# Passage from attention to experts: first early rows split beside the last heads, the last batch's rows on VectorE, late rows found over three tile steps, two gathers ahead of stores

## Chip, cores and metric

One core of a Trainium2 chip runs the whole kernel. The metric is the device time of one execution, in microseconds. Three runs of the kernel before gave 1546.72, 1548.99 and 1550.43 us; the median is 1548.99.

## What is computed

```python
# x, ctx: (16, 256, 256) float32; 8 heads of 128; 8 experts with 1024 hidden columns, 2 per token
x = x + tanh(g_xattn) * perceiver_attention(ctx, layernorm(x))   # keys: 256 context rows and 256 latent rows
n = layernorm(x)                                                 # eps 1e-5
gates = (n @ Wg + bg) / (1 + 1e-6)
weights, indices = top_k(gates, 2);  weights = softmax(weights)
h = silu(n @ W1[e] + b1[e]);  y = h @ W2[e] + b2[e]              # of the two chosen experts e
x = x + tanh(g_ffn) * sum(weights * y)
```

All of it is float32. A product on TensorE is made of three passes over parts that were split before: `hi` (rounded to the fast format, on ScalarE) and `lo` (the rest, on VectorE or POOL). Each operand of a product therefore passes ScalarE and then VectorE before TensorE can take it.

## The kernel before, in words

Each engine has its program in order (`sync`, `gpsimd`, `scalar`, `tensor`, `vector`), written out by hand; they meet at semaphores alone, so where an instruction stands in its engine's order is what sets when it runs.

**Attention.** 16 batches of 8 heads make `STEPS` = 128 steps i (L54), and two more drain them. In a step TensorE makes the scores of head i (`scores`), transposes the probabilities of head i-1 (`turn_probs`), projects head i-2 (`out_proj`) and works through units (`unit`): k, q and v parts of the next head, o of the last. VectorE reads maxima, the low halves `pt_lo`, kt, qt, v, ot; ScalarE the exponentials and high halves; POOL normalises the probabilities (L881). Behind the last head of a batch b the work on its rows is spread over the steps of the next batch: `residual` (h=1), `norm_rows` on POOL (h=1), the transposes t and gates g, `largest`, `choose`, `weigh` (h=6), `find_places` (h=7) on VectorE and `list_tokens` (h=7) on POOL, which writes the tokens' numbers into lists of each expert in DRAM with four indirect DMAs. The normalised rows go to `xhat_rows` in DRAM.

**Experts.** The pairs of token and expert are worked off in 40 tiles t: 31 wide ones of 256 rows (`WIDE`) and 9 of 128. The first five (`EARLY`) belong to the two fullest experts and take only rows of batches 0 to 13, so that they are known before attention ends; the others, the late ones, need the last batches. A wide tile has four steps n (`step_of(t)` = 4t). In step n TensorE does `hidden(n)` (12 products, W1) and `out(n - 2)` (12 products, W2); ScalarE does `silu(n)` and `hi_h(n)`, VectorE `lo_h(n)`. A tile's rows are gathered by POOL (`gather`, one DMA of 128 rows for each half), transposed by TensorE (`turn_x`, at the steps of `X_TURN`), split by ScalarE and VectorE (`hi_x`, `lo_x`, at those of `X_SPLIT`), and their weights taken (`take_weights`). When a tile is through, VectorE makes `finish` (bias, and a scaling of each 128x256 half by the weights, L1716) and POOL adds the rows to the output with an indirect DMA (`scatter`, L906); each scatter waits for the one before it (`s_add`).

**Beside it.** W2 of all experts is loaded (SP) and split in 32 pieces (`w2_hi`, `w2_lo`), the first four in steps 127 and 128 of attention (`W2_STEPS`), the others over the first expert steps; W1 of a tile is split two steps ahead of use (`w1_hi`, `w1_lo`). In steps 4 to 14 the last batch is dealt with: transposes t (step 4, waiting for the rows of `norm_rows(15)` on POOL), gates g, `choose`, r (step 7), `find_places(15)`, then `list_tokens(15)` on POOL, `find_rows` on VectorE (step 8, with `weigh(15)`), which says for each late row of tiles its expert and its place in the lists; POOL fetches the `names` (tokens) of the late rows, TensorE turns them at step 14 (`NAMES_STEP`), and VectorE writes the `token` table, on which `gather(5)`, the first late tile, waits.

**Around the change.** TensorE's order at attention step 127: `scores(127)`, `turn_probs(126)`, `out_proj(125)`, `turn_x(0)`, unit o(126); at step 128: `hidden(0)` (waits for `lo_x(0)`), `turn_probs(127)`, `out_proj(126)`, `hidden(1)`, o(127), `hidden(2)`; then `out_proj(127)`, `turn_x(1)`, `out(0)`, steps n from 3. POOL's order: at step 127 `normalise(127)`, `list_tokens(14)`; behind the loop `gather(2)` (two DMAs), `norm_rows(15)`, then by t: `gather(3)`, `scatter(0,0)`, `list_tokens(15)`; `scatter(0,1)`, `gather(4)`, `names`, `scatter(1,0)`; `scatter(1,1)`, `gather(5)`, and so on. A gather of tile t waits until tile t-2 is transposed and its weights are taken. In POOL's `norm_rows`, L821 is the variance with its epsilon, L793 the power to -1/2, L796 the sign, L799 the two instructions that write the rows. `turn_x(5)` stands at step 19, with `hi_x(5)` and `lo_x(5)`; step 20 is the first that uses them.

```python
X_TURN = ({step_of(t) + (t < WIDE) for t in range(1, N_TILES - 1) if t + 1 != EARLY} | {step_of(EARLY) - 1})
X_SPLIT = {step_of(t) + 2 for t in range(WIDE) if t + 1 != EARLY} | {step_of(EARLY) - 1}
```

## Time and profile before

| | |
|---|---|
| median of three runs | 1548.99 us (1546.72 to 1550.43) |
| the profiled execution's own time | 1550.09 us |
| its span, first to last instruction | 1548.4 us |
| mean granted TensorE clock | 0.993 of full speed |
| busy in the span | PE 97%, DVE 72%, ACT 62%, POOL 39% |
| attention | to about 1101 us; experts behind it |

The span holds all instructions of one execution; its own time lies 1.7 us above it. The granted clock has two levels in this trace, 1.0 (2.4 GHz) and 0.5 (1.2 GHz). Line numbers L... are those of the kernel before; products of all kinds stand at L181 to L183, so they are told apart by the tiles that they write: `score`, `ring` (units), `proj`, `ph` (hidden), `py` (out), `px` (turned rows; the first tile's go to `routing`). "Idle before" names what the profile saw end last. xt_lo is `lo_x`, ht_lo `lo_h`, w_lo `w2_lo`, w1s_lo `w1_lo`, and py with ht_lo is `out`.

### The profile page before, as it was taken

How to read it: one execution, taken by the hardware profiler on the slowest of the kernel's cores; microseconds unless marked ns; L12 is line 12 of the kernel's file. 1: busy time of each engine (PE TensorE's matmuls, PEld its weight loads, DVE VectorE, ACT ScalarE, POOL GpSimd, SP SyncE). 2: the span in 40 equal slices, each digit the busy share in tenths (PEclk: the TensorE clock that was granted, in tenths of full speed). 3: DMA queues.
4: the chain of work that ended last, by engine and by line, in shares of the span. 5: the costliest groups of instructions: out<-in, count | busy, mean ns of one | idle time of the engine just before them, and what ended most of it. 6: DMA issues, size and time to landing. Idle time of an engine off the chain costs nothing. (4 is left out here: it accounts for less than half of the span.)

```text
span 1548.4 us, 29904 instructions
## 1 busy us (share of the span) xinstructions
PE 1501.3 (97%) x10410; PEld 1383.4 (89%) x10410; DVE 1112.3 (72%) x2687; ACT 954.0 (62%) x2060; POOL 603.0 (39%) x714
## 2 busy tenths in 40 slices
PE   6999998999999999999999999999899999999997
PEld 5888897988989888898888889888889999999996
DVE  6777775777777777777777777677686666666685
ACT  5655654555555655655555555655677777777775
POOL 5323423233343333334243343233455444445442
PEclk9999999999999999999999999999999999999999
DMA  4000100000000000000000000012855545555553
GB/s 148 19 21 8 21 8 21 8 21 29 8 22 8 22 27 2 29 8 22 8 21 29 8 22 8 8 29 82 226 121 133 130 125 152 132 127 147 140 171 83
DMA packets 57823, 91.13 MB, mean 59 GB/s; under 512 B 8521, under 2 KB 44774, under 8 KB 57550
## 3 DMA queue, kind: packets, MB, share of 16 engines
q1 hardware_dynamic: 41710, 70.19, 14.1%
q0 software_dynamic: 15824, 18.98, 6.9%
q8 instruction: 88, 1.44, 0.4%
q14 instruction: 57, 0.47, 0.1%
q10 hardware_dynamic: 144, 0.05, 0.0%
HBM read 70.91 MB, written 18.29 MB: 58 GB/s over the span
## 5 line engine op out<-in xcount | busy, mean ns | idle before, releaser
L881 POOL TENSOR_SCALAR probs<-probs,rsum 128x512 f32<-128x512 f32 x256 | 174.2, 692 | 531.8 <-DVE rsum L1553 517.5
L1093 ACT ACTIVATE pt_hi<-turn 128x512 fp32r<-128x512 f32 x256 | 139.7, 597 | 238.5 <-PE turn L1239 238.5
L906 POOL DMA_INDIRECT out_rows<-yo,token x71 | 120.6, 1699 | 206.4 <-DMA out_rows<-yo,token 149.2
L1670 DVE TENSOR_TENSOR ht_lo<-hs,ht_hi 128x512 fp32r<-128x512 f32 x142 | 98.2, 692 | 119.8 <-ACT ht_hi L1058 114.9
L1547 DVE TENSOR_REDUCE smax<-score 128x1 f32<-128x512 f32 x256 | 169.8, 685 | 12.9 <-PE score L183 11.6
L992 ACT ACTIVATE probs<-score,nbias 128x512 f32<-128x512 f32 x256 | 173.7, 688 | 4.2 <-DVE nbias L1549 4.1
L1049 ACT ACTIVATE hs<-ph,vecs 128x256 f32<-128x256 f32 (+1 forms) x284 | 114.8, 460 | 95.1 <-PE ph L183 86.2
L1782 DVE TENSOR_TENSOR pt_lo<-turn,pt_hi 128x512 fp32r<-128x512 f32 x256 | 164.2, 682 | 9.3 <-ACT pt_hi L1093 9.2
L181 PE MATMUL py<-w_hi,ht_lo 128*128 (+1 forms) x568 | 163.1, 287 | 3.9 <-DVE ht_lo L1670 3.9
L182 PE MATMUL py<-w_lo,ht_hi 128*128 (+1 forms) x568 | 161.0, 283 | 0.0
L183 PE MATMUL py<-w_hi,ht_hi 128*128 (+1 forms) x568 | 161.0, 283 | 0.0
L181 PE MATMUL ring<-pt_hi,v_lo 128*128 128x256 f32 x512 | 146.4, 286 | 9.4 <-DVE kt_lo L1450 7.7
L980 ACT ACTIVATE kt_hi<-ring,vecs 128x512 fp32r<-128x512 f32 x128 | 88.6, 692 | 94.4 <-PE ring L183 93.7
L181 PE MATMUL ph<-xt_hi,w1s_lo 128*128 128x256 f32 x496 | 141.4, 285 | 4.6 <-DVE xt_lo L1648 4.5
L183 PE MATMUL ring<-pt_hi,v_hi 128*128 128x256 f32 x512 | 145.1, 283 | 0.0
L182 PE MATMUL ring<-pt_lo,v_hi 128*128 128x256 f32 x512 | 144.9, 283 | 0.0
L1450 DVE SCALAR_TENSOR_TENSOR qt_lo<-ring,vecs,qt_hi 128x256 fp32r<-128x256 f32 x128 | 61.8, 483 | 107.6 <-ACT qt_hi L982 104.9
L183 PE MATMUL ph<-xt_hi,w1s_hi 128*128 128x256 f32 x496 | 139.0, 280 | 0.0
L182 PE MATMUL ph<-xt_lo,w1s_hi 128*128 128x256 f32 x496 | 138.7, 280 | 0.0
L1239 PEld LDWEIGHTS turn<-ident,probs 128*128 128x128 f32 x1024 | 121.4, 142 | 17.4 <-POOL probs L881 0.3
L1239 PE MATMUL turn<-ident,probs 128*128 128x128 f32 x1024 | 134.4, 275 | 0.0
L1450 DVE SCALAR_TENSOR_TENSOR kt_lo<-ring,vecs,kt_hi 128x512 fp32r<-128x512 f32 x128 | 95.8, 748 | 51.0 <-ACT kt_hi L980 43.1
(247 smaller groups left out, 4708.8 us busy)
## 6 DMA issues: line engine op xcount, KB each, us to landing
w_raw<-in_L_ffn_W SPq DMA_DIRECT2D x45, 1024.0 KB, 8.4
xhat_rows<-rows SPq DMA_DIRECT2D x16, 264.0 KB, 2.2
x_raw<-in_x SPq DMA_DIRECT2D x16, 256.0 KB, 3.0
c_raw<-in_ctx SPq DMA_DIRECT2D x16, 256.0 KB, 3.1
out_rows<-x SPq DMA_DIRECT2D x16, 256.0 KB, 2.2
xg<-xhat_rows,token POOLq DMA_INDIRECT x71, 5.0
out_rows<-yo,token POOLq DMA_INDIRECT x71
v_raw<-in_L_xattn_Wkv SPq DMA_DIRECT2D x2, 512.0 KB, 8.3
```

The costliest lines, as they stand in the source:

```text
L181: pe.matmul(out, ll, rh, start=start, stop=False, **kw)
L182: pe.matmul(out, lh, rl, start=False, stop=False, **kw)
L183: return pe.matmul(out, lh, rh, start=False, stop=stop, **kw)
L881: last = pool.tensor_scalar(probs[n % 2][:, t, :], probs[n % 2][:, t, :], rsum[:, n % 2, t:t + 1], 1.0, ALU.mult, ALU.mult)
L906: pool.indirect_dma_start(out=A["out"], out_offset=bass.IndirectOffsetOnAxis(ap=token[:, u:u + 1].bitcast(U32), axis=0), in_=yo_of(t)[:, s ...
L992: act.activation(probs[n % 2][:, t, :], score[t][:, :], ACT.Exp, scale=SCALE, bias=nbias[:, n % 2, t:t + 1], accum_out=ssum[:, n % 2, t:t ...
L1049: last = act.activation(by_step(hs[n % N_HS], t)[:, g, :], by_step(ph[n % N_PH] if t < WIDE else turned_of(n), t)[:, g, :], ACT.Silu, bias ...
L1093: act.activation(pt[0][:, 2 * t:2 * t + 2, :], turn[t][:, :].rearrange("p (j i) -> p j i", j=2), ACT.Copy).then_inc(s_pthi, 1)
L1239: last = pe.transpose(turn[t][:, j * T + q * P:j * T + (q + 1) * P], probs[n % 2][:, q, (2 * t + j) * P:(2 * t + j + 1) * P], ident[:, :])
L1450: dve.scalar_tensor_tensor(out=lo[:, :], in0=part, scalar=bias, in1=hi[:, :].bitcast(F32), op0=ALU.add, op1=ALU.subtract).then_inc(s_read, 1)
L1547: own.mark(dve.tensor_reduce(smax[:, n % 2, t:t + 1], score[t][:, :], AX_X, ALU.max))
L1782: dve.tensor_tensor(pt[1][:, 2 * t:2 * t + 2, :], turn[t][:, :].rearrange("p (j i) -> p j i", j=2), pt[0][:, 2 * t:2 * t + 2, :].bitcast(F ...
```

## The change

1. On TensorE `turn_x(0)` moves ahead of `turn_probs(126)`; on ScalarE `hi_x(0)` and the first two `w2_hi` move ahead of the high half of o(126); on VectorE `lo_x(0)` moves ahead of the low half of o(126). `find_places(14)` moves from attention step 127 to 128, behind `lo_h(0)`, and the weights of tiles 0 and 1 are taken at step 128.
2. The last batch's rows are normalised by VectorE, inside its order behind `residual(15)` and `lo_h(1)`; POOL keeps only the power, behind `gather(2)`. A semaphore `ve_last` is new.
3. `find_rows` becomes `count_rows` (step 8) and `find_late_rows` (step 9); `weigh(15)` moves to step 10.
4. On POOL `gather(3)` and `gather(4)` both stand ahead of `scatter(0,0)`, and `list_tokens(15)` and the fetch of `names` ahead of `scatter(0,1)`.
5. `turn_x(5)`, `hi_x(5)` and `lo_x(5)` move from step 19 to step 18.

```diff
@@ -129,8 +129,8 @@
 NAMES_STEP = 14
 
 
-X_TURN = ({step_of(t) + (t < WIDE) for t in range(1, N_TILES - 1) if t + 1 != EARLY} | {step_of(EARLY) - 1})
-X_SPLIT = {step_of(t) + 2 for t in range(WIDE) if t + 1 != EARLY} | {step_of(EARLY) - 1}
+X_TURN = ({step_of(t) + (t < WIDE) for t in range(1, N_TILES - 1) if t + 1 != EARLY} | {step_of(EARLY) - 2})
+X_SPLIT = {step_of(t) + 2 for t in range(WIDE)}
 
 
 def plan_units():
@@ -481,6 +481,7 @@
         s_whi = sem("weights_hi")
         s_wlo = {"dve": sem("weights_lo_dve"), "pool": sem("weights_lo_pool")}
         s_media0, s_zt1 = sem("kvt0_media"), sem("zt0_media")
+        s_ve_last = sem("ve_last")
         s_ve0, s_rs0 = sem("ve0"), sem("rs0")
         s_z0, s_zt0, s_lat0, s_kvl0 = sem("z0_latents"), sem("z0_turned"), sem("zt0_latents"), sem("kvt0_latents")
         s_tg = sem("tanh_gate")
@@ -938,7 +939,8 @@
 
             for s in range(SUB):
                 gather(2, s)
-            norm_rows(B - 1)
+            pool.wait_ge(s_ve_last, 1)
+            pool.tensor_tensor(rs_c[:, 0:TT], ve["c"][:, 0:TT], minus_half[:, 0:TT], ALU.pow).then_inc(s_rsc, 1)
             for t in range(1, N_TILES + 1):
                 if WIDE + N_XG <= t + N_GN < N_TILES:
                     gather(t + N_GN, 0)
@@ -947,19 +949,21 @@
                 if t + N_XG == EARLY:
                     pool.wait_ge(s_rowst[1], 16 * (B // 2))
                     pool.wait_ge(s_token, 1)
-                if t + N_XG < min(N_TILES, WIDE + N_XG):
-                    for s in range(subs(t + N_XG)):
-                        gather(t + N_XG, s)
-                if t == 2:
+                for later in {1: (3, 4), 2: ()}.get(t, (t + N_XG,)):
+                    if later < min(N_TILES, WIDE + N_XG):
+                        for s in range(subs(later)):
+                            gather(later, s)
+                if t == 1:
+                    scatter(0, 0)
+                    list_tokens(B - 1)
                     pool.wait_ge(s_row, 1)
                     pool.wait_ge(s_listed, 16 * TOP * TT * B)
                     pool.indirect_dma_start(
                         out=names[0:LATE_SUB, 0:P], out_offset=None, in_=dram["lists"],
                         in_offset=bass.IndirectOffsetOnAxis(ap=row[0:LATE_SUB, :].bitcast(U32), axis=0),
                     ).then_inc(s_names, 16)
-                scatter(t - 1, 0)
-                if t == 1:
-                    list_tokens(B - 1)
+                if t > 1:
+                    scatter(t - 1, 0)
             pool.wait_ge(s_add, 16 * ROWS)
 
         @program("scalar")
@@ -1101,6 +1105,10 @@
                 if i < STEPS:
                     exp(i, 0)
                     exp(i, 1)
+                if i == STEPS - 1:
+                    hi_x(0)
+                    for q in W2_STEPS[i]:
+                        w2_hi(q)
                 for u in units:
                     if u[0] != "k":
                         hi_part(*u)
@@ -1117,13 +1125,13 @@
                 if i % H == E_STEP and 1 <= i // H < B:
                     exp_gap(i // H - 1)
                 if i == STEPS - 1:
-                    hi_x(0)
                     e = expert_of(act, 0)
                     act.wait_ge(s_x2st[0], 16 * (B // 2))
                     act.wait_ge(s_rowst[0], 16 * (B // 2))
                     act.activation(warm[:, :], iota8[:, :], ACT.Silu).then_inc(s_warm, 1)
-                for q in W2_STEPS.get(i, ()):
-                    w2_hi(q)
+                if i == STEPS:
+                    for q in W2_STEPS[i]:
+                        w2_hi(q)
             piece = W2_BEFORE
             for n in range(1, FIRST_N):
                 t, j = TILE_OF[n]
@@ -1358,14 +1366,14 @@
                     scores(i)
                 if i == STEPS:
                     hidden(0)
-                if 1 <= i <= STEPS:
-                    turn_probs(i - 1)
-
-                if STEPS - 1 <= i <= STEPS:
-                    out_proj(i - 2)
                 if i == STEPS - 1:
                     wait_read(pe, order[number["o", STEPS - 1] - 2])
                     turn_x(0)
+                if 1 <= i <= STEPS:
+                    turn_probs(i - 1)
+
+                if STEPS - 1 <= i <= STEPS:
+                    out_proj(i - 2)
                 if i == STEPS:
                     hidden(1)
                 for u in steps[i]:
@@ -1583,7 +1591,7 @@
                 for i, n in enumerate(HOME_SUB):
                     own.mark(dve.tensor_scalar(begin[:, i:i + 1], begin[:, i:i + 1], float(n), None, ALU.add))
 
-            def find_rows():
+            def count_rows():
 
                 def do(instruction):
                     own.mark(instruction)
@@ -1609,6 +1617,14 @@
                                             op0=ALU.mult, op1=ALU.subtract))
                 own.mark(dve.tensor_tensor(begin[:, ODD:ODD + E], begin[:, 0:E], length[:, 0:E], ALU.add))
                 do(dve.tensor_reduce(wide_rows[:, :], length[:, 0:E], AX_X, ALU.add))
+
+            def find_late_rows():
+
+                def do(instruction):
+                    own.mark(instruction)
+                    own.wait()
+
+                own.wait()
                 do(dve.tensor_scalar(wide_rows[:, :], wide_rows[:, :], -1.0, float(LATE_WIDE), ALU.mult, ALU.add))
                 do(dve.tensor_scalar(length[:, GAP:GAP + 1], wide_rows[:, :], 0.0, None, ALU.max))
                 do(dve.tensor_tensor_scan(end[:, :], length[:, :], zero[:, :], 0.0, ALU.add, ALU.add))
@@ -1785,11 +1801,14 @@
                             .then_inc(s_ptlo, 1)
                 if i == STEPS:
                     lo_h(0)
+                    find_places(B - 2)
                 for u in steps[i]:
                     if u[0] in "kq":
                         read_unit(*u)
                 if i < STEPS:
                     reciprocal_sum(i)
+                if i == STEPS - 1:
+                    lo_x(0)
                 for u in steps[i]:
                     if u[0] in "vogr":
                         read_unit(*u)
@@ -1804,7 +1823,7 @@
                 if 1 <= b < B:
                     for at, part in ((R_STEP, residual), (G_STEP, largest), (E_STEP, choose), (W_STEP, weigh),
                                      (L_STEP, find_places)):
-                        if h == at:
+                        if h == at and i != STEPS - 1:
                             part(b - 1)
                 if i == HOME_STEP:
                     find_home()
@@ -1813,15 +1832,21 @@
                     dve.tensor_copy(token[:, 0:EARLY_SUB], early_names[:, :]).then_inc(s_early_token, 1)
                 if W1_STEP <= i < W1_STEP + PARTS:
                     w1_lo(0, i - W1_STEP)
-                if i == STEPS - 1:
-                    lo_x(0)
                 for q in W2_STEPS.get(i, ()):
                     w2_lo(q)
-                if i == STEPS - 1:
+                if i == STEPS:
                     take_weights(0)
                     take_weights(1)
             residual(B - 1)
+            dve.wait_ge(s_mvc, B)
+            dve.tensor_scalar(ve["c"][:, 0:TT], mv_c[:, 0:TT, 1], 1.0, EPS, ALU.mult, ALU.add).then_inc(s_ve_last, 1)
             lo_h(1)
+            dve.wait_ge(s_rsc, B)
+            dve.wait_ge(s_rowst[(B - 1) % 2], 16 * ((B - 1) // 2))
+            for t in range(TT):
+                last = dve.tensor_scalar(rows[(B - 1) % 2][:, t, 0:D], x2[(B - 1) % 2][:, t, :], mv_c[:, t, 0:1],
+                                         rs_c[:, t:t + 1], ALU.subtract, ALU.mult)
+            last.then_inc(s_xn, 1)
             piece = W2_BEFORE
             for n in range(2, FIRST_N):
                 t, j = TILE_OF[n]
@@ -1842,7 +1867,10 @@
                     largest(B - 1)
                     choose(B - 1)
                 if n == 8:
-                    find_rows()
+                    count_rows()
+                if n == 9:
+                    find_late_rows()
+                if n == 10:
                     weigh(B - 1)
                 if n == NAMES_STEP:
                     fill_tables()
```

## Rows read from the trace of the kernel before

**Rows 1.** The page: busy time and share of the engines; the gathers' median to landing.

```profile
PE 1501.3 (97%) x10410; PEld 1383.4 (89%) x10410; DVE 1112.3 (72%) x2687; ACT 954.0 (62%) x2060; POOL 603.0 (39%) x714
...
xg<-xhat_rows,token POOLq DMA_INDIRECT x71, 5.0
```

**Rows 2.** Stretches: width, busy us (instructions) of PE, PEld, DVE, ACT, POOL; clock, DMA.

```profile
1092.00:1095.40 3.40, 3.40 (x19) 3.40 (x18) 2.17 (x11) 1.44 (x3) 2.79 (x3) 0.50 1.09 350
1163.80:1167.00 3.20, 3.20 (x16) 3.20 (x16) 1.92 (x5) 1.52 (x4) 2.90 (x2) 0.50 0.30 85
1200.00:1300.00 100.00, 100.00 (x852) 100.00 (x851) 62.90 (x133) 73.04 (x146) 47.79 (x34) 1.00 0.49 130
1130.00:1142.70 12.70, 9.57 (x77) 8.96 (x77) 12.44 (x31) 8.21 (x18) 8.63 (x5) 1.00 0.58 67
```

**Rows 3.** Waits of TensorE, 1050 to 1200 us: total, times, longest.

```profile
PE ph L181 <- DVE xt_lo L1648: 4.5, 2, 2.8
...
PE py L181 <- DVE ht_lo L1670: 1.6, 1, 1.6
PE px L1263 <- DMA xg<-xhat_rows,token: 1.4, 1, 1.4
PE ring L1206 <- POOL rows L799: 1.3, 1, 1.3
```

**Rows 4.** Timeline of TensorE: start, duration in us; in brackets the idle time before.

```profile
1090.81 0.39 PE L181 MATMUL ph<-xt_hi,w1s_lo 128*128 128x256 f32 x1 [2.77 <-DVE xt_lo L1648]
...
1106.23 0.28 PE L181 MATMUL ph<-xt_hi,w1s_lo 128*128 128x256 f32 x1
...
1111.72 0.63 PE L1263 MATMUL px<-ident,xg 128*128 128x128 f32 x4
...
1167.40 0.60 PE L1263 MATMUL px<-ident,xg 128*128 128x128 f32 x4
```

**Rows 5.** Timeline of ScalarE around the last heads.

```profile
1088.08 0.48 ACT L984 ACTIVATE ot_hi<-ring,vecs 128x256 fp32r<-128x256 f32 x1 [1.50 <-PE ring L183]
...
1090.47 1.14 ACT L1023 ACTIVATE w_hi<-w_raw 128x512 fp32r<-128x512 f32 x2
```

**Rows 6.** Timeline of VectorE: places, residual and moments, scaling of rows.

```profile
1090.00 0.17 DVE L1507 CAST place<-placef 128x4 int32<-128x4 f32 x1
...
1101.52 0.69 DVE L1532 TENSOR_TENSOR y<-proj,bo 128x512 f32<-128x512 f32 x1
...
1103.82 0.25 DVE L1417 BATCH_NORM_AGGREGATE mv_c<-stats_c 128x2 f32<-128x6 f32 x2
...
1119.43 0.62 DVE L1716 TENSOR_SCALAR yo<-yo,wcol 128x256 f32<-128x256 f32 x2
...
1136.63 1.28 DVE L1716 TENSOR_SCALAR yo<-yo,wcol 128x256 f32<-128x256 f32 x2
```

**Rows 7.** Timeline of POOL: gather(2), the power, gather(4), a store.

```profile
1097.43 0.96 POOL L892 DMA_INDIRECT xg<-xhat_rows,token  x1 [0.30 <-issue]
...
1104.77 0.72 POOL L793 TENSOR_TENSOR rs_c<-ve_c,minus_half 128x2 f32<-128x2 f32 x1
...
1131.24 1.00 POOL L892 DMA_INDIRECT xg<-xhat_rows,token  x1 [0.30 <-issue]
...
1160.08 1.58 POOL L906 DMA_INDIRECT out_rows<-yo,token  x1 [8.17 <-DMA out_rows<-yo,token]
```

**Rows 8.** POOL's DMA queue in 1102-1106, 1106-1108, 1108-1112, 1112-1116, 1162-1166: packets, MB, share.

```profile
q0 software_dynamic: 39, 0.11, 23.7%
...
q0 software_dynamic: 59, 0.16, 19.6%
...
q0 software_dynamic: 5, 0.01, 0.8%
...
q0 software_dynamic: 95, 0.27, 17.9%
...
q0 software_dynamic: 232, 0.40, 52.8%
```

More of the change, by code:

```diff
@@ L1360, in _ @@
                     hidden(0)
+                if i == STEPS - 1:
+                    wait_read(pe, order[number["o", STEPS - 1] - 2])
+                    turn_x(0)
                 if 1 <= i <= STEPS:
@@ L1365, in _ @@
                     out_proj(i - 2)
-                if i == STEPS - 1:
-                    wait_read(pe, order[number["o", STEPS - 1] - 2])
-                    turn_x(0)
                 if i == STEPS:
@@ L1792, in _ @@
                     reciprocal_sum(i)
+                if i == STEPS - 1:
+                    lo_x(0)
                 for u in steps[i]:
@@ L1815, in _ @@
                     w1_lo(0, i - W1_STEP)
-                if i == STEPS - 1:
-                    lo_x(0)
                 for q in W2_STEPS.get(i, ()):
                     w2_lo(q)
-                if i == STEPS - 1:
+                if i == STEPS:
                     take_weights(0)
```

## The prediction

> **What bounds the kernel now.** I read the page's busy shares first: TensorE is busy for 97% of the span [rows 1]. The table of stretches comes next. In it the reader is to see where TensorE has no reserve: from 1200 us on it is busy all the time at the full granted clock [rows 2], so that every microsecond won before that comes off the end, and nothing else in the kernel has to be looked at. The waits of TensorE between 1050 and 1200 us then name what is there to win in the passage to the experts: 4.5 us in two waits for the low half of turned rows (2.8 and 1.7), 1.6 for a low half of hidden values, 1.4 for a gather, 1.3 for the last batch's normalised rows on POOL [rows 3]. Behind the 2.8 and the 1.7 the granted clock was 0.50, that is 1.2 GHz instead of 2.4, for 3.4 and 3.2 us [rows 2]: 1.7 and 1.6 us more of lost time. In all some 12 us, of which the change aims at each piece. The timelines of the engines say what each piece hangs on; the steps n of the experts are about 2.9 us each.
>
> **First early rows split beside the last heads.** In before, TensorE ended its last but one attention unit at 1088.0 and stood until 1090.81 for lo_x(0) [rows 4]. ScalarE had been free since 1086.6 (1088.08 less 1.50 idle), but read the turned rows only behind ot_hi, 0.59 long [rows 5]. Now the transposes (0.4) stand ahead of the probabilities' and push ScalarE's two exponentials back by about 0.25. hi_x(0) runs 1086.8 to 1087.35 and lo_x(0), 0.7 long, ends at 1088.05. Step 0 starts at 1088.1: 2.7 us won, and the 1.7 of half clock behind it with it. The two w2 pieces that ScalarE now does ahead of ot_hi (1.14 [rows 5]) move that by 0.3, hidden by the transposes ahead of the projection that reads it. So TensorE is through with attention 4.4 us earlier, at about 1096.7 instead of 1101.1.
>
> **What is late next.** find_places(14), which before ended at 1090.2 [rows 6], now stands behind lo_h(0), which needs step 0, the last head's two pt_hi on ScalarE (behind its table load, ready at 1090.3), the activation (0.85) and hi_h(0) (0.64). Durations without a group are those of the same timelines' neighbouring lines. I get 1093.0 for lo_h(0)'s start, 1093.55 for its end and, with 1.15 for the eight small instructions, 1094.7: 4.5 us later than before. POOL has list_tokens(14) and gather(2) queued behind it and issues six DMAs, which before took from 1090.2 to 1098.4 [rows 6, 7]; now they end at 1102.9, and only then can POOL take the power of the new s_ve_last. The power (0.72 [rows 7]) gives rs_c at 1103.7. VectorE meanwhile: low half of the last head 1095.4, two w2 pieces 1.2, four take_weights 1.1, residual and moments 2.5 (1101.52 to 1104.07 [rows 6]), the spread 0.2, lo_h(1) 0.6, done by 1101.4. It then **stands 2.3 us in the new wait for rs_c**, with lo_x(1), lo_h(2) and, through them, TensorE behind it. out(1) needs lo_h(1): a wait of about 1.4. The two row instructions on VectorE replace 2.9 us of POOL, but their price is not shown as such: the nearest row is the scaling of two 128x256 tiles with a per-partition scalar, 0.62 for both while POOL was idle and 1.28 while POOL issued DMAs [rows 6]. POOL goes on to gather(3) here, so I take 1.28 and keep 0.62 as the other end. Rows are ready at 1105.0, lo_x(1) at 1105.7; step 4 starts then, against 1106.23 [rows 4], with a wait of about 2.7. Of 4.4 us only 0.5 is left.
>
> From step 4 to turn_x(2) took 5.5 us (1106.23 to 1111.72), 1.3 of them the wait for POOL's rows [rows 3, 4], which is gone: 4.2, so turn_x(2) is wanted at 1109.9. Two things push it back. The waits of 1.4 and 2.7 lie like those ahead of the first half-clock stretch, which was 1.7: between nothing and 1.7. And gather(2): it is issued 4.5 us later, the last part at 1101.9. Before, it was issued by 1097.43, and POOL's queue moved 0.11 MB in 1102 to 1106 and 0.16 in 1106 to 1108, together the 0.27 MB of its two tiles: 10 us to land. In 1108 to 1112 that queue got 0.8% of the engines while the w2 loads kept them full [rows 8]. Bounds for its landing: 1106.5, if the loads are through by then (5 us from issue, the median of all 71 gathers [rows 1]), and 1112 (the same 10 us). I take 1110 and, with part of the half clock, turn_x(2) at 1110.7: **1.0 us won**.
>
> The Trainium skill, DMA: Bandwidth & Descriptors, Queues, rings and completion order, says that each DMA engine goes round the queues that have work, a packet at a time. By that gather(2) would get turns beside the loads and land without a wait of TensorE; POOL's 0.8% against the loads' fill does not look like equal turns, so the measurement has the word. By the rule turn_x(2) would start 0.8 earlier than in my sum, which is the first step of case (a) below.
>
> **Late rows over three pairs, gathers ahead of stores.** VectorE has no time free here: it is busy 12.44 of 12.70 us from 1130 to 1142.7 [rows 2]. Steps 8 to 10 hold the same instructions in another order, so the waits of 1.6 (low half) and 1.4 (gather(4), issued at 1131.24 behind the lists and a store [rows 3, 7], now some 12 us sooner) go, but I expect new ones of 0.9 and 2.2 at steps 12 and 13, where VectorE's w1 piece is late behind weigh and finish. Only 0.6 us that VectorE stood because of the gather is really won: the token table comes 1.0 + 0.6 = 1.6 us sooner. The names are fetched ahead of one store instead of behind it and have room. POOL's queue past them: four stores wait for each other, about 5 us each, so the tile behind the names is still on time.
>
> **The first late tile turned at step 18.** Its wait of 1.7 and the 1.6 of half clock behind it go, provided gather(5) has landed: its issue hangs on the tokens, 10 us ahead of step 18, enough for the 5 us that it takes. TensorE would thus reach turn_x(6) 1.6 + 3.3 = 4.9 us sooner than 1167.40 [rows 4]. But gather(6) stands behind a store that waited 8.17 us for the one before it, in the stretch of w1 and b2 loads [rows 7]; tokens, loads and stores all shift together by 1.6. In 1162 to 1166 POOL's queue moved 0.40 MB, one store (0.13) and gather(6) (0.27) [rows 8]: it had landed at about 1166.3, 1.1 ahead of its use. So turn_x(6) can start at 1164.7, **2.7 us won**, with TensorE idle 2.2 before it. Waits of 1.4 and 1.6 left the clock alone, 1.7 and 2.8 didn't [rows 2, 3]: this one is at the edge, and I charge half of 1.6.
>
> **Sum.** 2.7 - 0.8 = 1.9, say 2.0 us off the profiled execution, 1550.09 (span 1548.4 and 1.7 around it): 1548.1. That execution is 1.1 above the median of the three runs, 1548.99, so I forecast 1547.0. About 0.2% (3 us) is what a measurement of this kernel can tell from no change.
>
> **Rivals.** (a) *The passage clears*, over 3.1 us: loads are through before gather(2) wants the engines, no half-clock stretch is left, and POOL is free of gather(2) sooner than I have it. turn_x(2) is then at 1109.3 (rows at the short price, 0.62), 2.4 won, the tokens 3.0 sooner, turn_x(6) 4.1 won; with a faster store chain up to 6. That gives 1545 to 1543. For it: the w2 loads keep their old start, and six of POOL's DMAs leave their way until 1095. Against: VectorE's queue is full [rows 2], and hides no part of a wait. (b) *Slower*: gather(2), issued behind find_places(14), is caught by the starved stretch of 1108 to 1112 [rows 8] and lands at 1115.6, as the next gather did (0.27 MB in 1112 to 1116 [rows 8]). turn_x(2) is then 3.9 late; the 0.6 and 1.1 are still won, and a half clock behind the wait costs 1.6: 3.8 slower, 1552.8. It decides from a landing past about 1111.7, and costs over 0.2% from 1114.8 on. (c) *It doesn't do what it says*: the rows on VectorE wait for POOL anyhow, so moving them brings nothing; that is in my sum (0.5 of 4.4 left), and with both half-clock stretches kept the whole change brings 0 to 1: 1548 to 1549.
>
> **Chances.** My forecast with (c) 0.57, (a) 0.33, (b) 0.10, counted as slower throughout. The range takes the whole of the first (1545.9 to 1549.8), most of (a) and the near end of (b): 1543.6 to 1550.2.
>
> **What would show it.** Right: first matmul of step 0 at about 1088.1 behind a wait below 0.2; place of batch 14 at about 1094.7; a wait of VectorE for POOL's rs_c of 2 us or more, and of TensorE for lo_x(1) ahead of step 4; the wait for rows on POOL gone; a wait of 2 us for a gather ahead of turn_x(6). Wrong: no wait of VectorE for rs_c, turn_x(2) before 1108 or behind 1113, or turn_x(6) before 1163.

## The result, and the profile after

The changed kernel takes 1556.61 us (median of four runs, 1556.17 to 1558.17), the kernel before beside it 1547.86. The ratio is 1.0057, with a 95% interval of 1.0041 to 1.0073: 8.7 us slower, where 2 us faster were forecast and 1550.2 was the end of the range. The profiled execution took 1558.17 us with a span of 1556.5, 8.1 us over the span of before; its mean granted clock is 0.991 against 0.993.

The busy line of the page, then the waits of TensorE between 1050 and 1200 us (total, times, longest), of the changed kernel; they answer to [rows 1, 3]:

```profile
PE 1501.4 (96%) x10410; PEld 1385.0 (89%) x10410; DVE 1111.0 (71%) x2690; ACT 950.7 (61%) x2060; POOL 599.3 (39%) x710
```

```profile
PE px L1271 <- DMA xg<-xhat_rows,token: 10.0, 2, 6.3
PE ph L181 <- DVE xt_lo L1664: 2.9, 2, 2.7
PE ph L181 <- DVE w1s_lo L1670: 2.0, 1, 2.0
PE ring L181 <- issue: 1.7, 2, 1.0
PE py L181 <- DVE ht_lo L1686: 1.1, 1, 1.1
```

TensorE's work is the same; the waits changed hands. Those that the change aimed at went: the rows on POOL (1.3), the low hidden half (1.6) and both waits for turned rows (4.5 together). In their place stand one of 2.65 for lo_x(1), one of 2.0 for w1s_lo, and 10.0 us for gathers, where it was 1.4.

The timeline of TensorE shows where. Until the last heads each instruction of this trace stands 1.72 us earlier than in the one of before (the same matmul at 1084.67 and 1086.39), so 1.72 is to be added before a time is put beside [rows 4]; such a time is called aligned below.

```profile
1084.67 0.35 PE L181 MATMUL ring<-pt_hi,v_lo 128*128 128x256 f32 x1 [1.04 <-issue]
...
1094.36 0.60 PE L1271 MATMUL px<-ident,xg 128*128 128x128 f32 x4
...
1099.06 0.38 PE L181 MATMUL py<-w_hi,ht_lo 128*128 128x256 f32 x1 [1.09 <-DVE ht_lo L1686]
...
1103.40 0.58 PE L181 MATMUL ph<-xt_hi,w1s_lo 128*128 128x256 f32 x1 [2.65 <-DVE xt_lo L1664]
...
1112.73 0.44 PE L1271 MATMUL px<-ident,xg 128*128 128x128 f32 x2 [3.63 <-DMA xg<-xhat_rows,token]
...
1162.90 0.69 PE L1271 MATMUL px<-ident,xg 128*128 128x128 f32 x2 [6.32 <-DMA xg<-xhat_rows,token]
...
1174.12 0.38 PE L1271 MATMUL px<-ident,xg 128*128 128x128 f32 x2
```

The gap ahead of step 0 is gone. turn_x(2) (1112.73) starts at 1114.45 aligned, 2.7 later than before, behind 3.63 us for gather(2). turn_x(5) (1162.90, now at step 18) waits 6.32 for gather(5), where before it did not wait at all. turn_x(6) (1174.12) is at 1175.84 aligned: 8.4 later, nearly the whole loss (the last tiles, behind 1461 us, add some 1.3). Behind the waits the clock fell to its lower level, as the stretches show (columns as in [rows 2]):

```profile
1103.40:1106.40 3.00, 3.00 (x14) 3.00 (x15) 2.95 (x5) 0.00 (x0) 1.36 (x1) 0.50 0.82 76
1162.90:1167.50 4.60, 4.60 (x22) 4.60 (x23) 1.07 (x5) 1.46 (x4) 1.71 (x2) 0.50 0.25 29
```

They cost 1.5 and 2.3 us. Behind turn_x(2) it was 0.58 over 3.3 us as well. POOL's timeline in the changed kernel has both lost gathers in it:

```profile
1093.17 1.08 POOL L859 DMA_INDIRECT expert_lists<-ids,place  x1 [6.57 <-DVE place L1515]
...
1098.43 1.45 POOL L893 DMA_INDIRECT xg<-xhat_rows,token  x1 [0.30 <-issue]
1100.19 0.96 POOL L893 DMA_INDIRECT xg<-xhat_rows,token  x1 [0.30 <-issue]
1101.17 0.74 POOL L943 TENSOR_TENSOR rs_c<-ve_c,minus_half 128x2 f32<-128x2 f32 x1
...
1130.65 1.12 POOL L859 DMA_INDIRECT expert_lists<-ids,place  x1 [0.30 <-issue]
1138.10 1.70 POOL L961 DMA_INDIRECT names<-expert_lists,row  x1 [6.33 <-DMA expert_lists<-ids,place]
1140.10 1.62 POOL L907 DMA_INDIRECT out_rows<-yo,token  x1 [0.30 <-DVE yo L1732]
1144.77 3.53 POOL L907 DMA_INDIRECT out_rows<-yo,token  x1 [3.05 <-DMA out_rows<-yo,token]
1151.09 1.77 POOL L907 DMA_INDIRECT out_rows<-yo,token  x1 [2.79 <-DMA out_rows<-yo,token]
1153.16 1.03 POOL L893 DMA_INDIRECT xg<-xhat_rows,token  x1 [0.30 <-issue]
```

gather(2) goes out behind the four list writes of batch 14. Further down, POOL stands 6.33 us in the wait ahead of the names; then come three stores, one behind the other, and only then gather(5), at 1153.16. SP's two loads of w1 and the one of b2 went out at 1149.82 to 1151.55, ahead of it.

### The profile page after: what moved, and what is told of

The parts are those of the page before. It is cut to its first block, busy times and chain, and to the rows that moved or that the text cites. A ratio compares the mean times of both kernels' runs of the same rounds, so it can differ in the third digit from the quotient of the medians.

```text
span 1556.5 us, 29904 instructions
## 1 busy us (share of the span) xinstructions
PE 1501.4 (96%) x10410; PEld 1385.0 (89%) x10410; DVE 1111.0 (71%) x2690; ACT 950.7 (61%) x2060; POOL 599.3 (39%) x710
## 4 chain that ended last, share of the span: by engine, by line
PE 81%; DVE 8%; DMA 4%; ACT 3%; issue 2%; POOL 0%; another core or an unknown queue 0%; ACTq 0%; DVEq 0%; POOLq 0%
PE ring L181 12%; PE ring L182 12%; PE ring L183 12%; PE turn L1247 6%; PE score L181 4%; PE score L183 3%; PE score L182 3%; PE py L181 3%; PE ph L181 3%; PE ph L183 3%; PE ph L182 3%; PE py L182 3%; PE py L183 3%; DMA out_rows<-yo,token 2%; PE proj L182 2%
```

## The experiments

The parts of the change are called by number: 1, first early rows beside the last heads (with the places of batch 14 moved to step 128); 2, the last batch's rows on VectorE; 3, late rows over three pairs; 4, POOL's order (gathers ahead of stores, names ahead of scatter(0,1)); 5, tile 5 turned at step 18. They ran on four chips, four experiments to a chip, beside runs of the kernel before on the same chip (medians 1547.19, 1554.09, 1558.56, 1551.39 us): only the ratios are compared, 0.001 being 1.55 us. A ratio is of medians, a trace shows one execution. In five kernels the profiled one lies 2.5 us or more off the median: places back (1551.48 against 1554.01), part 4 alone (1555.78 against 1562.86), gather(2) first (1557.24 against 1560.24), loads split with POOL's order as before (1559.74 against 1556.57) and writes behind on the changed kernel (1549.46 against 1552.88). There the waits quoted need not be those of the median.

### Two places undone

**Store first.** The changed kernel with one store ahead of the wait for the names:

```diff
-                if t >= 2 and subs(t - 2) == 2:
+                if t >= 3 and subs(t - 2) == 2:
                     scatter(t - 2, 1)
...
                 if t == 1:
                     scatter(0, 0)
                     list_tokens(B - 1)
+                    scatter(0, 1)
                     pool.wait_ge(s_row, 1)
```

> The changed kernel with one edit: scatter(0,1) goes out behind the four list writes and ahead of the wait for the names, as before the change. Theory (store chain): in the changed kernel POOL stood 6.3 us for the list writes to land with scatter(0,1) queued behind that wait, and as each store waits for the one before it, gather(5) went out at 1153.2, 5 us behind the token table, in the w1 and b2 loads. Then gather(5) now goes out within 1 us of the token table, the wait ahead of turn_x(5) falls from 6.3 to under 1.5 us, and the time from 1556.6 to 1549 to 1551. Rival (gather(5) is late because of the loads alone, or because it is wanted a step sooner): the wait stays at 4 us or more and the time above 1554.

Ratio 1.0054 (1.0034 to 1.0073). The wait went as expected, and the gain did not come. gather(5) is issued at 1148.46, ahead of the loads (1149.46), and turn_x(5) has no wait at all; but the wait is passed on:

```profile
1168.66 1.11 PE L1272 MATMUL px<-ident,xg 128*128 128x128 f32 x4 [3.47 <-DMA xg<-xhat_rows,token]
```

gather(6) is now the late one, with half clock behind it: turn_x(7) comes 14.6 us after turn_x(6), not 11.75.

**Places back.** find_places(14) at step 127 again:

```diff
-                    find_places(B - 2)
...
-                        if h == at and i != STEPS - 1:
+                        if h == at:
```

> The changed kernel with one edit: find_places(14) stands at attention step 127 again, behind the low half of o(126) and behind lo_x(0). Theory (late places): the list writes and gather(2) go out 4 to 4.5 us sooner, VectorE's wait for the power of rs_c (2.95) and TensorE's for lo_x(1) (2.65) nearly go, and the wait for gather(2) (3.6) falls under 1; the wait ahead of turn_x(5) stays at 6 us, so the time falls by 3 to 5 us, to 1552 to 1554. Rival (gather(2) is held by the w2 loads whenever it goes out): the wait for gather(2) stays above 2.5 us and the time within 1.5 us of 1556.6.

Ratio 1.0039 (1.0023 to 1.0055). The waits for rs_c and for lo_x(1) nearly went (0.6 us instead of 2.95, and 0.26 instead of 2.65), as the prediction's sum has them. The wait for gather(2) stayed, 2.99 us. This trace stands 2.01 us ahead of the changed kernel's at the last heads; with that added, the list writes went 4.4 us earlier and gather(2) only 2.3, and it landed 4.1 earlier: 19.9 us behind the first list write (1086.72 to 1106.58), where it was 19.6 in the changed kernel (1093.17 to 1112.73). The landing follows the writes and not its own issue.

**Both.** The two edits together:

> Both edits, store first and places back. If the two causes are separate and are all that went wrong, the waits for gather(2) and gather(5) are both under 1.5 us and the time is 1544 to 1547, below the 1547.9 of the kernel before. If something else in the change costs time, it stays above 1548.5.

Ratio 1.0032 (1.0018 to 1.0047); turn_x(2) waits 3.07, and turn_x(5) again 5.96. One of POOL's stores took 6.94 us to issue here (1136.94) and pushed gather(5) behind the loads once more.

**gather(3) held.** Whether gather(3), which now follows at once, takes the engines from gather(2):

```diff
+                if t == 1:
+                    pool.wait_ge(s_px, 3)
                 for later in {1: (3, 4), 2: ()}.get(t, (t + N_XG,)):
```

> The changed kernel with one edit: POOL issues gather(3) only when turn_x(2) has run, instead of right behind gather(2). Theory (late places alone): no difference, the wait ahead of turn_x(2) stays at 3.6 us and the time at 1556 to 1557. Rival (gather(3), two DMAs of 128 rows just behind it, slows gather(2)): that wait falls by 2 us or more and the time by 2 to 4.

Ratio 1.0064 (1.0043 to 1.0085), turn_x(2) waits 2.94: 0.7 us less, and nothing gained. gather(3) is not the cause.

### Each part alone, on the kernel before

The edits are those of the diff.

> The kernel before with part 1 of the change alone (first early rows split beside the last heads, find_places(14) at step 128). Theory (the split wins 4.4 us and gives them back, and more, because the list writes and gather(2) follow find_places(14)): gather(2) lands some 19 us behind batch 14's places, as in the first four runs, so that TensorE waits for it 3 us or more ahead of turn_x(2); the wait for POOL's rows grows from 1.3 to 3 or 4 us. Time 1548.5 to 1551. Rival (the split is a gain, the loss is in the other parts): 1543 to 1546.

Part 1: ratio 1.0025 (1.0009 to 1.0041). The gap ahead of step 0 is gone, turn_x(2) waits 3.78 for gather(2), and TensorE 3.19 for POOL's rows. So the part that wins 2.8 us at its own place loses 3.9 over all.

> The kernel before with part 4 alone (gather(3), gather(4), scatter(0,0), lists, names, scatter(0,1) on POOL). Theory (a store behind the names' wait): names go out 6 us behind the last list write as before, scatter(0,1) 5 us later than before, and with it the chain of stores, so that gather(5) goes out about 1151 instead of 1147.2, behind the w1 and b2 loads; TensorE waits for it 2 to 5 us at step 19, the wait of 1.4 for gather(4) is gone: 1549 to 1552. Rival (POOL's order is neutral or a small gain): 1545.5 to 1547.5.

Part 4: ratio 1.0048 (1.0032 to 1.0064). Names behind a wait of 6.79 us, gather(5) issued at 1153.74 behind the loads of 1148.57, turn_x(5) waits 3.88 though it stands at step 19 still. This trace is of the fastest execution of seven, so the 7.4 us of the ratio are not all in it.

> The kernel before with part 2 alone (the last batch's rows on VectorE). The wait for POOL's rows (1.3) goes, VectorE waits 1 to 1.5 us for the power, and step 4 starts up to 1 us later: within 1 us of the kernel before by every theory, 1546 to 1548.5. More than 2 us slower would put a cause here that I have not seen.

Part 2: ratio 0.9995 (0.9983 to 1.0006): nothing, as rival (c) had it for this piece. The wait for POOL's rows went and the one for gather(4) fell to 0.8; 0.3 and 0.6 us came elsewhere.

> The kernel before with part 5 alone (first late tile turned and split at step 18). gather(5), issued ahead of the loads, has landed by step 18, the wait of 1.7 for lo_x(5) goes; TensorE then waits 2 to 4 us for gather(6) ahead of turn_x(6), whose landing is unchanged. Theory (gathers set the pace, not the split): within 1.5 us of the kernel before, 1545.5 to 1548.5. Rival (the step is wanted too early and gather(5) has not landed): a wait for gather(5) of 2 us or more and 1549 or more.

Part 5: ratio 1.0045 (1.003 to 1.0061). The wait ahead of lo_x(5) is gone with its half clock, and turn_x(6) waits 9.88 us. POOL's timeline says why: the first of gather(6)'s two DMAs took 6.02 us to issue, with no transfer under way from 1164 to 1168.

```profile
1161.68 6.02 POOL L892 DMA_INDIRECT xg<-xhat_rows,token  x1 [0.30 <-issue]
1168.00 0.97 POOL L892 DMA_INDIRECT xg<-xhat_rows,token  x1 [0.30 <-issue]
```

Over the first 5.1 of these 6 us VectorE ran subtractions of two tensors in SBUF (two w_lo, w1s_lo, ht_lo) without a pause, up to 1166.81; the issue ended at 1167.70.

The four parts add up to 1.1% against 0.57% for the whole. Parts 4 and 5 make neighbouring gathers late, gather(5) and gather(6), and in the changed kernel turn_x(6), behind the wait for gather(5), has none of its own; that the waits overlap is read from this, and the two parts were not run as a pair. Nor was part 3 run alone. The changed kernel's own rows suggest its price: 2.0 us for w1s_lo, for 1.6 (ht_lo) taken away.

**The long issue.** Part 5 alone, VectorE standing until gather(6) is issued:

```diff
...
+                if t + N_XG == 6:
+                    pool.memset(lists["flag"][:, :], 0.0).then_inc(s_issued, 1)
...
+                if n == 19:
+                    dve.wait_ge(s_issued, 1)
                 while piece < w2_by(n):
                     w2_lo(piece)
```

> Part 5 alone, as in the run before, with one addition: at step 19 VectorE stands still until POOL has issued both DMAs of gather(6) (a 4-element memset of POOL behind them gives the sign). Theory H (the issue is held): in the run of part 5 alone POOL's first DMA of gather(6) took 6.02 us from 1161.68 to 1167.70 instead of 1.0, and over those 6 us VectorE ran only subtractions that read two tensors from SBUF, without a pause; POOL gets to write its descriptors only where VectorE leaves it a gap. Then both DMAs take 1.0 to 1.5 us each here, VectorE stands about 2 to 3 us at step 19 (it had 5 to spare), turn_x(6) waits 9.88 - 5 = about 5 us or less, and the ratio falls from 1.0045 to 1.001 to 1.003. Rival (the issue is slow on its own, its queue being full or the indices slow to read): the first DMA takes about 6 us again, VectorE stands 6 us more, turn_x(6) waits 10 or more, ratio 1.005 or above.

Ratio 0.9999 (0.9987 to 1.0012): with both issues short the loss of part 5 is gone, and more of it than expected. turn_x(6) waits 2.00.

```profile
1168.44 1.04 POOL L894 DMA_INDIRECT xg<-xhat_rows,token  x1 [0.30 <-issue]
1169.78 1.46 POOL L894 DMA_INDIRECT xg<-xhat_rows,token  x1 [0.30 <-issue]
1171.23 0.13 POOL L956 MEMSET flag<- 128x4 f32 x1
```

VectorE stood only 0.99 us in its new wait, and only at 1170.4, while the first issue, short too, lay under its subtractions. So the run shows that the loss of part 5 goes with the long issue, and not that the pause is what shortened it. More can be said from all traces of this case. Of the 1008 DMA issues of POOL that start between 1050 and 1250 us, 23 took 2.9 us or more. Each of them lay under a run of VectorE's subtractions without a pause (at 73% or more of its length, and at 64% or more under those with both operands in SBUF), and each ended just behind the end of that run: 20 of them 0.82 to 0.89 us behind it, three 1.42 to 1.55. So such an issue lasts until VectorE's run ends. But 96 others lay to 90% or more under subtractions of two tensors in SBUF and took under 1.9. A run of subtractions is what the long ones have in common, and it doesn't suffice.

### What holds gather(2)

The prediction's reason for a late gather(2) was SP's loads. The next kernels tell these from the list writes.

**Loads split.** The changed kernel with three of the six w2 loads some 10 us later:

```diff
-                    for at in range(2, E):
+                    for at in range(2, 5):
                         load_w2(at)
...
                 sp.dma_start(ov[b], x2[b % 2][:, :, :]).then_inc(s_x2st[b % 2], 16)
+                if b == B - 1:
+                    for at in range(5, E):
+                        load_w2(at)
```

> The changed kernel with three of the six w2 loads of 1 MB (experts 5 to 7) moved behind the store of the last x, some 10 us later. Theory S (the list writes and gather(2), in POOL's queue, are starved by SP's loads): the writes and the gather get their share at about 1095 instead of 1104; gather(2) lands by 1106 instead of 1112.7, turn_x(2)'s wait of 3.63 us goes or falls under 1, no half clock there; turn_x(5) still waits 6 us or more; ratio 1.0057 - 0.0025 = about 1.003. Rival (the list writes of 4 bytes are slow by themselves, 6 to 7 us behind the last of them even on an empty queue): gather(2) lands at 1110 or later, the wait stays over 2, ratio 1.005 to 1.006.

Ratio 1.0051 (1.0035 to 1.0067), turn_x(2) waits 4.75: the loads that were moved are not the cause. The list writes are issued at 1101.97 to 1106.91, and gather(2) lands at 1121.27, 19.3 us behind the first. The DMA queues in 1106 to 1108, 1108 to 1110 and 1110 to 1112 of this run (packets, MB, share of the 16 engines' time):

```profile
q1 hardware_dynamic: 150, 0.14, 252.5%
q0 software_dynamic: 44, 0.00, 1.6%
...
q1 hardware_dynamic: 8, 0.01, 28.6%
...
q1 hardware_dynamic: 9, 0.01, 41.0%
```

q1 is SP's queue, which moves 0.7 MB in 2 us otherwise. Here 44 packets of 32 and 4 bytes pass on POOL's queue, the end of the four list writes. Behind them hardly a packet of either queue is finished for 6 us, though home_b2, the store of the last x and gather(2) were issued by 1110, with the next loads behind them; packets of SP's queue that take 0.06 us otherwise were under way for up to 6.0. So it looks as if the writes hold the loads, and not the loads the writes; the run without the writes, below, shows it.

**gather(2) first.** The kernel before with parts 1 (places where they were) and 2, gather(2) ahead of the writes:

```diff
...
+                if i == STEPS - 1:
+                    for s in range(SUB):
+                        gather(2, s)
                 if h == L_STEP and 1 <= b < B:
                     list_tokens(b - 1)
...
```

> Kernel before with part 1 (but the places of batch 14 found where they were) and part 2, and with gather(2) ahead of the list writes of batch 14 in POOL's order. TensorE reaches tile 0's rows without its gap as in part 1. Theory O (order in POOL's queue decides when gather(2) lands): it is issued at about 1094.5, as soon as turn_x(0) has read its buffer, lands by 1103, turn_x(2) does not wait; tile 5's gather stands as in the kernel before; ratio 0.997 to 0.999, faster than the kernel before for the first time. Rival (the loads starve it wherever it stands): it lands at 1106 or later, turn_x(2) waits 2 to 3 us with half clock behind, ratio 1.000 to 1.003.

Ratio 1.0014 (1.0002 to 1.0026): neither theory gave this trace. gather(2) landed in time and turn_x(2) did not wait; but rs_c's power was now behind the four writes in POOL's order (1110.98), and step 4 waited 5.21 us for lo_x(1), which needs it.

**Loads split, POOL's order as before**, on the same kernel:

> As the run before this one, but with POOL's order as in the kernel before (list writes ahead of gather(2)) and three of the six w2 loads behind the store of the last x instead. Theory S: list writes at about 1087, gather(2) issued at 1094 to 1096 and landed by 1102, turn_x(2) does not wait, ratio 0.997 to 0.999. Rival (4-byte writes slow by themselves): the gather lands at 1104 to 1107, turn_x(2) waits 1 to 3 us, ratio 1.000 to 1.002. In both a wait may come later where TensorE, ahead by 3 to 4 us, meets gather(4) or tile 5's gather.

Ratio 0.9979 (0.9966 to 0.9992): the time that theory S gave, by a trace that it didn't: gather(2) landed 18.1 us behind the first write, and turn_x(2), turn_x(4) and turn_x(6) waited 1.25, 2.69 and 2.47. With the places where they were and the loads not split it was 19.9 us, in the two runs with the places back, so the loads may add up to 1.8 of them; those kernels differ in more than the loads.

**Writes behind.** List writes of batch 14 behind rs_c's power and gather(3), on that kernel with the loads in their old place (the kernel before, parts 1 and 2, the places where they were):

```diff
-                if h == L_STEP and 1 <= b < B:
+                if h == L_STEP and 1 <= b < B and i != STEPS - 1:
                     list_tokens(b - 1)
...
                     for s in range(subs(t + N_XG)):
                         gather(t + N_XG, s)
+                if t == 1:
+                    list_tokens(B - 2)
```

> Kernel before with part 1 (places of batch 14 found where they were) and part 2; POOL's order is gather(2), rs_c's power, gather(3), then the list writes of batch 14. Theory W (four list writes hold every transfer behind them for 6 to 8 us): gather(2) and rs_c are free of them, turn_x(2) does not wait, xt_lo of step 4 waits under 1 us (5.21 in the run of gather(2) first), ratio 0.996 to 0.998. Rival (SP's loads starve POOL's queue): turn_x(2) waits 1 to 3 us, ratio 0.999 to 1.001.

Ratio 0.9973 (0.9962 to 0.9983), the fastest of this study: 1546.55 against 1551.39 us. TensorE's waits from 1050 to 1200 us in it:

```profile
PE py L181 <- DVE ht_lo L1678: 3.6, 2, 2.5
PE ph L181 <- DVE xt_lo L1656: 2.1, 2, 1.8
PE ring L181 <- issue: 1.7, 2, 1.0
PE px L1271 <- DMA xg<-xhat_rows,token: 0.4, 1, 0.4
```

Gathers cost 0.4 us here, 1.4 in the kernel before and 10.0 in the changed one, and the 2.77 of [rows 4] stay won.

**The same on the changed kernel:**

> The changed kernel with the list writes of batch 14 behind gather(3) instead of ahead of gather(2). Theory W: gather(2) is issued at about 1094.5, as soon as its buffer is free, and lands by 1103; turn_x(2)'s wait of 3.63 us and its half clock go; turn_x(5) still waits about 6 us, since the names and the stores are as they were; ratio 1.0057 - 0.0025 = about 1.003. Rival (the loads starve it): gather(2) lands at 1106 or later and half of the wait or more stays, ratio 1.004 to 1.006.

Ratio 1.0008 (0.9999 to 1.0017): 0.0049 less, 7.6 us back for one list moved, where theory W (the four list writes hold what stands behind them) gave 0.0025. turn_x(2)'s wait is gone, and so is the one for lo_x(1), since rs_c is free of the writes as well (step 4 waits 0.26). With POOL free sooner, tokens and stores move up too, and turn_x(5) waits 2.14 instead of 6.32, turn_x(6) 2.12. The names still stand 6.46 us.

**No writes.** The changed kernel without the list writes of batch 14; the two waits that count list writes are lowered with them:

```diff
-                if h == L_STEP and 1 <= b < B:
+                if h == L_STEP and 1 <= b < B and i != STEPS - 1:
                     list_tokens(b - 1)
...
```

> The changed kernel without the four list writes of batch 14: its pairs of tokens and experts are in no list, so their rows are missing from the late tiles; everything else runs. The six w2 loads stand in SP's queue as they did. Theory W: the DMA engines move 0.6 to 0.7 MB in each 2 us until the loads are done (with the writes it fell to 0.4 and then 0.1), gather(2) is issued at about 1094 and lands 6 to 8 us later, by 1102; no wait at turn_x(2). Rival (the loads starve POOL's queue): gather(2) lands only once the loads are done, at 1105 to 1108, as in the run with the places back. Ratio about 1.003 in both, so the profile decides.

Ratio 1.0 (0.9988 to 1.0012), and the profile decides for theory W. All DMA packets in ten microseconds of the changed kernel (1098 to 1108), and in about the same ten of this one (1102 to 1112, its trace standing 3.3 later):

```profile
DMA packets 1802, 1.74 MB, mean 174 GB/s; under 512 B 155, under 2 KB 1790, under 8 KB 1800
```

```profile
DMA packets 3057, 3.40 MB, mean 340 GB/s; under 512 B 154, under 2 KB 2929, under 8 KB 3055
```

Twice the bytes, with SP's loads as before. POOL's timeline of this run, and TensorE's turn_x(2):

```profile
1099.19 1.03 POOL L893 DMA_INDIRECT xg<-xhat_rows,token  x1 [9.26 <-DVE wjunk L1703]
1100.52 0.96 POOL L893 DMA_INDIRECT xg<-xhat_rows,token  x1 [0.30 <-issue]
```

```profile
1108.45 0.64 PE L1271 MATMUL px<-ident,xg 128*128 128x128 f32 x4
```

gather(2)'s packets passed from 1103.9 to 1106.6, 7 us behind its issue and in the midst of the loads, and TensorE did not wait.

**All together.** The fastest kernel with part 4's order, but one store ahead of the names:

> The first kernel of this call with part 4's order too, but scatter(0,1) ahead of the names, and without parts 3 and 5: gather(3), list writes of 14, gather(4), scatter(0,0), list writes of 15, scatter(0,1), names, scatter(1,0), (1,1), gather(5). Theory W: no wait at turn_x(2), none at turn_x(4) (2 to 2.7 us in the runs of parts 1 and 2), gather(5) issued ahead of or just beside SP's loads of tile 5 and 6, at turn_x(5) 0 to 3 us; ratio 0.994 to 0.997. Rival (a store or a gather is late next, as after every gain so far): turn_x(5) or turn_x(6) waits 4 us or more with half clock behind, ratio 0.998 to 1.001.

Ratio 0.9983 (0.997 to 0.9996): no wait for any gather, and not faster than without part 4. gather(4)'s wait of 0.41 was all that part 4 had left to win.

## Why the prediction was wrong

**Right**, within 0.7 us (aligned): the start of step 0 (its gap of 2.77 us is gone); the places of batch 14 (1094.44, forecast 1094.7); VectorE's new wait for rs_c (2.95, forecast 2.3); out(1)'s wait (1.09, forecast 1.4); the new wait ahead of step 4 (2.65 at 1105.12, forecast 2.7 at 1105.7); the wait for w1s_lo (1.99, forecast 2.2). The wait of 0.9 expected ahead of it came as 0.28. For the two row instructions I took 1.28 us, and they took 0.79, nearer to the other end. The half clock behind the waits came, 1.5 us.

**First step that failed: "Bounds for its landing: 1106.5 ... and 1112 ... I take 1110".** gather(2) landed at 1114.45 aligned, past both ends, 3.8 us late against the forecast turn_x(2). The row of q0's 0.8% share in 1108 to 1112 [rows 8] was read as POOL's queue losing to SP's. It is no such sign: gather(3) was all that stood in that queue then, its two DMAs issued only at 1109.04 and 1110.43, and even with no writes ahead gather(2)'s first packet came 4.7 us behind its issue. The sign stood some us earlier in the trace of before, in SP's queue in 1100 to 1102, 1102 to 1104 and 1104 to 1106, where it moves 0.7 MB in 2 us otherwise:

```profile
q1 hardware_dynamic: 171, 0.17, 112.2%
...
q1 hardware_dynamic: 178, 0.18, 81.5%
...
q1 hardware_dynamic: 139, 0.14, 39.6%
```

What the runs show is that the four list writes ahead of gather(2) hold both queues: half the loads moved away left its landing 19.3 us behind the first write (19.6 in the changed kernel), the writes left out doubled the bytes moved. Seen so, the landing could be forecast: in the nine kernels where TensorE waited for it behind the writes, whether the places were moved or not, it came 18.1 to 19.9 us behind the first write (in before its last packet passed 17.9 us behind it), and the change moved that write back. Rival (b) came nearer, at 10%, with the landing at 1115.6 and turn_x(2) 3.9 us later than before (measured 1114.45 and 2.7), but with the wrong cause; its price, 1552.8, is also not what the run shows.

**Second, and larger: the names "have room ... so the tile behind the names is still on time".** The names need the last list writes landed, 6.3 to 7.7 us behind the last issue (6.33 here, 6.31 to 7.72 in the six experiments with this order). Before, POOL filled this time with scatter(0,1) and gather(4); with gather(4) moved ahead and the store behind, it stands. The stores wait for each other, about 5 us each, so all of it reaches gather(5), which in the end falls behind SP's loads; one of the stores also took 3.53 us to issue. I had counted the room in front of the names and not what stands behind them. turn_x(5) lost 6.32 us and, by half clock, 2.3.

**Third: "it had landed at about 1166.3", held fixed while TensorE came 4.9 us sooner to turn_x(6).** The landing of gather(6) is no date. It hangs on the chain of stores: in the changed kernel it is issued at 1169.98 aligned, 8.0 later than before, and with the store first 3.2 later, where TensorE waits 3.47 for it. It also hangs on how long the issue takes: part 5 alone waits 9.88 us, not 2.2, with an issue of 6.02 us, and 2.00 where the issue was short. In the changed kernel TensorE is later still and does not wait for gather(6), so this step is no term of its 8.7 us. The kernel before has a mild case of it, a gather(4) DMA of 2.68 us instead of 1.0, beside the stretch in which VectorE is busy 12.44 of 12.70 us [rows 2]; that row was used for VectorE and not for POOL.

**Size.** Of the 11.1 us by which turn_x(6) missed its forecast (1175.84 against 1164.7), 3.8 were there at turn_x(2); the other 7.4 came by turn_x(6): 8.6 at turn_x(5) and 1.6 at the lower clock behind turn_x(2) (turn_x(3) is 4.3 later than before, turn_x(2) 2.7), less what was won between. That part 4's wait and part 5's early turn share their price is suggested by the sum of the parts; how the 8.7 us divide among them is not settled.

What stays open: why the four writes hold the engines. They were moved and left out, never made larger or fewer; whether it is their size, their number or the spread of their addresses was not tried. Nor is it known what else it takes for an issue of POOL to become long.

## What to carry to other kernels

Put what the critical engine waits for ahead of small scattered writes in DMA order, on whatever queue: of all that this change moved, the position worth most was the list writes' in front of a gather and of the power that gives rs_c (7.6 us in the changed kernel). Before work is taken out from between a DMA and the wait on it, ask how long the DMA takes to land and what was filling that time. Treat the landing of a transfer as the end of its own chain: an engine that arrives earlier does not find it earlier. And where POOL issues DMAs beside a long run of VectorE's subtractions, allow for an issue that can last until the run ends.

## What the runs showed of the hardware

- **Small writes hold both queues.** Behind four indirect DMAs of 128 writes of 4 bytes SP's queue, which moves 0.7 MB in 2 us otherwise, moved 0.14, 0.01 and 0.01 in the run with the loads split, and 0.59, 0.40, 0.38, 0.12, 0.19 and 0.24 from 1098 to 1110 in the changed kernel: a stop of some 6 us there, a slow stretch of over 10 here. With nothing else in the queues their landing is signalled 6.3 to 7.7 us behind the last issue, though their packets end within 2. The Trainium skill, DMA: Bandwidth & Descriptors, Specifications, says that below 512 bytes the engines read, modify and write. That fits slow writes; no run here shows that it is the reason. The turn by turn of its section Queues, rings and completion order, which the prediction weighed, can't be seen in these stretches, and does fit the run without the writes: there gather(2) passed amid the loads.
- **The same writes stop SP too.** Its two small home_b2 loads took 10.56 us to issue behind them, with all six w2 loads ahead of both, and 4.3 to 10 in the other runs of that order; 3.6 to 3.9 in the five where no writes stood ahead of gather(2).

```profile
1099.69 10.56 SPq L754 DMA_DIRECT2D home_b<-in_L_ffn_b  x2
```

- **An indirect DMA's issue took from 0.9 to 6.9 us**, and the 23 of 2.9 us or more all ended 0.8 to 1.6 us behind a run of VectorE's subtractions, most of them of two tensors in SBUF. The Trainium skill, GPSIMD Engine Reference, Key points, names this contention, for instructions with two inputs in SBUF; the trace agrees, and gives it a size: a store of 3.53 us in the changed kernel, a gather of 6.02 with part 5.
- **The clock.** Behind the waits of 2.65, 3.63 and 6.32 us of the changed kernel it was at or near the lower level (0.50, 0.58 and 0.50 of 2.4 GHz, over 3.0, 3.3 and 4.6 us). A wait's length alone doesn't tell what follows. In the run with the loads split and POOL's order as before, 1.25 us ahead of turn_x(2) were followed by 0.55 over 3 us, and in the fastest kernel 1.81 us ahead of lo_x(5) by 0.55 over 3.7. But 2.48 us at 1129.65 in that kernel left it at 1.00, and so did 2.66 at 1112.18 with the loads split in the changed kernel and 2.77 at 1098.75 in the run with the pause. The edge between 1.6 and 1.7 us, on which the prediction charged half for a wait of 2.2, is thus none.
